# Column sums over features: high and low parts stacked on 64 partitions each, one pass with ones

## The reference

```python
def rmsnorm(x, w):
    return x * jax.lax.rsqrt(jnp.mean(x * x, axis=-1, keepdims=True) + EPS) * w
def film(x, cond, w, b):
    scale, shift = jnp.split(cond @ w + b, 2, axis=-1)
    return x * (1.0 + scale[:, None, :]) + shift[:, None, :]
h = film(rmsnorm(x, norm1_w), cond, film1_w, film1_b)
Q, K, V = h @ q_w + q_b, h @ k_w + k_b, h @ v_w + v_b
attn = softmax(einsum('bnd,bmd->bnm', Q, K) * 512 ** -0.5)
x = x + (einsum('bnm,bmd->bnd', attn, V) @ proj_w + proj_b)
h = film(rmsnorm(x, norm2_w), cond, film2_w, film2_b)
out = x + (gelu(h @ mlp_w1 + mlp_b1) @ mlp_w2 + mlp_b2)
```

## Time and profile before

| | us |
|---|---|
| median of 3 timed runs | 1762.76 (1762.69 to 1762.88) |
| profiled execution, its own time | 1765.63 |
| its span, first to last instruction | 1763.8 |
| TensorE busy | 1750.1 (99%) |
| VectorE busy | 1254.7 (71%) |
| ScalarE busy | 888.1 (50%) |
| GpSimd busy | 205.7 (12%) |

### The profile page before, as it was taken

The page is one execution under the profiler, slowest core; times in us unless marked ns, Lnnn a source line. Parts: engine busy times, 40 slices in busy tenths (PEclk is TensorE's granted clock), DMA queues, the critical chain, the costliest instruction groups (busy, mean ns, idle before and its releaser), DMA issues.

```text
span 1763.8 us, 23169 instructions
## 1 busy us (share of the span) xinstructions
PE 1750.1 (99%) x8308; PEld 1468.9 (83%) x8308; DVE 1254.7 (71%) x1749; ACT 888.1 (50%) x1490; POOL 205.7 (12%) x202
## 2 busy tenths in 40 slices
PE   8899999999999999999999999999999999999998
PEld 7788888888888888888888888888888888888887
DVE  5867677565665787588578758858875885885476
ACT  5454545545454555455455445545544554653344
POOL 0578685000000000000000000000000000000000
PEclk9999999999999999999999999999999999999999
DMA  9586868633226678768777866876786677677675
GB/s 335 163 297 249 291 256 274 245 99 112 78 102 199 201 250 277 207 203 276 249 197 250 280 202 207 274 248 197 262 267 201 220 269 243 191 244 240 193 233 194
DMA packets 202307, 395.83 MB, mean 224 GB/s; under 512 B 24145, under 2 KB 28241, under 8 KB 200145
## 3 DMA queue, kind: packets, MB, share of 16 engines
q1 hardware_dynamic: 202192, 394.34, 68.8%
HBM read 331.25 MB, written 62.98 MB: 224 GB/s over the span
## 4 chain that ended last, share of the span: by engine, by line
PE 96%; DMA 2%; DVE 1%; ACT 1%; SPq 0%; POOL 0%; issue 0%; DVEq 0%
PE psum L687 35%; PE psum L707 23%; PE psum L587 14%; PE psum L715 12%; PE psum L657 3%; PE psum L615 3%; PE psum L616 3%; PE psum L620 3%; DMA norm_row<-rs_scratch 1%; DMA rs_scratch<-rstd 1%; DMA x_tok<-x_dram 1%; DVE h L1053 0%; ACT x_tok L803 0%; PE psum L601 0%; PE psum L648 0%; DVE h L1046 0%
## 5 line engine op out<-in xcount | busy, mean ns | idle before, releaser
L687 PE MATMUL psum<-op_hi_P,ring 128*128 128x512 f32 x1792 | 552.0, 389 | 0.0
L707 PE MATMUL psum<-stage_hi,ring 128*128 128x512 f32 x1792 | 442.5, 389 | 0.0
L707 PEld LDWEIGHTS psum<-stage_hi,ring 128*128 128x128 f32 x1792 | 336.3, 188 | 69.8
L687 PEld LDWEIGHTS psum<-op_hi_P,ring 128*128 128x128 f32 x1792 | 336.1, 188 | 69.6
L888 ACT CAST stage_hi<-x 128x1024 fp32r<-128x1024 f32 x224 | 235.4, 1054 | 235.2 <-PE psum L707 223.0
L687 PE MATMUL psum<-op_lo_P,ring 128*128 128x512 f32 x896 | 348.6, 389 | 0.0
L1266 DVE TENSOR_TENSOR stage_lo<-x,stage_hi 128x1024 fp32r<-128x1024 f32 x224 | 273.6, 1225 | 72.3 <-ACT stage_hi L888 72.1
L872 ACT ACTIVATE x<-x,vecs 128x512 f32<-128x512 f32 x192 | 138.1, 723 | 283.9 <-DVE x L1253 283.9
L715 PE MATMUL psum<-stage_lo,ring 128*128 128x512 f32 x896 | 239.5, 389 | 0.0
L687 PEld LDWEIGHTS psum<-op_lo_P,ring 128*128 128x128 f32 x896 | 168.2, 188 | 35.0
L715 PEld LDWEIGHTS psum<-stage_lo,ring 128*128 128x128 f32 x896 | 168.2, 188 | 34.9
(11 more groups left out here) (154 smaller groups left out, 2240.4 us busy)
## 6 DMA issues: line engine op xcount, KB each, us to landing
ring<-wu_scratch SPq DMA_DIRECT2D x448, 256.0 KB, 3.1
ring<-wd_scratch SPq DMA_DIRECT2D x448, 256.0 KB, 2.9
x_tok<-x_dram SPq DMA_DIRECT2D x16, 1024.0 KB, 10.9
xT_in<-xT_dram SPq DMA_DIRECT2D x16, 1024.0 KB, 8.2
x2T_scratch<-xT_in SPq DMA_DIRECT2D x32, 512.0 KB, 3.4
hn<-x2T_scratch SPq DMA_DIRECT2D x32, 512.0 KB, 5.6
xres<-x2T_scratch SPq DMA_DIRECT2D x32, 512.0 KB, 5.0
out_dram<-xres SPq DMA_DIRECT2D x32, 512.0 KB, 4.4
```

The source lines that it names most:

```text
L687: mm = pe.matmul(to, wt, b, start=q in FRESH and t == 0, stop=t == len(steps) - 1, skip_group_check=True)
L707: mm = pe.matmul(bank(q, dt), a[:, dt, part, :], stage_hi[r][:, e, :], start=q in FRESH and ss == 0 and e == 0 and part == 0, stop=False, ...
```

## The change

After the last accumulation VectorE now folds the upper 64 partitions onto the lower 64: one more addition, of 64x512 for the key terms and of 64x1024 for the sums of squares, which waits for the operation before it. A wait for the fold itself stands behind it at the end of `key_terms` and of `add_squares`. ScalarE casts the folded 64 partitions into the lower half of one tile (`key_halves`, `sq_halves_*`), and VectorE writes the low part into the upper half of the same tile. TensorE then sums both with one matmul with ones instead of two. `key_terms` no longer waits for `key_row_full`, since the low part has left the memory of `key_bias`.

```diff
@@ -631,7 +632,7 @@
                 pe.wait_ge(key_hi_done, n + 1)
                 pe.wait_ge(key_lo_done, n + 1)
                 wait_used(pe, pT_read, n)
-                product(pT, [(ones_r[:], key_hi[:]), (ones_r[:], key_lo[:])], key_row_full)
+                product(pT, [(ones_r[:], key_halves[:])], key_row_full)
 
             def scores(n):
                 pe.wait_ge(g_read, GB * n + GB)
...
@@ -658,13 +659,13 @@
                                    start=True, stop=True)
                 mm.then_inc(out_full, 1)
 
-            def sum_features(m, hi, lo, into):
+            def sum_features(m, halves, into):
 
                 pe.wait_ge(sq_hi_done, m + 1)
                 pe.wait_ge(sq_lo_done, m + 1)
                 for f in range(2):
                     t = slice(TOK * f, TOK * f + TOK)
-                    product(into[f], [(ones_r[:], hi[:, t]), (ones_r[:], lo[:, t])], stat_full if f == 1 else None)
+                    product(into[f], [(ones_r[:], halves[:, t])], stat_full if f == 1 else None)
 
             def up(p, jj, q):
                 s, w = jj % 2, stream(p, 0, 7 * jj + UP_ORDER.index(q))
...
@@ -820,9 +821,9 @@
                 nc.scalar.copy(h_hi[m % 2][:, k, :], h[m % 2][:, k, :]).then_inc(h_hi_done, 1)
 
             def key_high(n):
-                act.wait_ge(key_done, KD * n + KD)
+                act.wait_ge(key_done, (KD + 1) * n + KD + 1)
                 wait_used(act, key_row_full, n)
-                nc.scalar.copy(key_hi[:], key_bias[:]).then_inc(key_hi_done, 1)
+                nc.scalar.copy(key_halves[0:HALF_P, :], key_bias[0:HALF_P, :]).then_inc(key_hi_done, 1)
 
             def keep_g(n, j):
                 act.wait_ge(g_full, GB * n + j + 1)
...
@@ -845,9 +846,9 @@
                     act.wait_ge(hn_loaded[k], 16 * m + 16)
                     nc.scalar.activation(into[:, k, :], hn[:, k, :], ACT.Square).then_inc(sq_done, 1)
 
-            def sums_high(m, squares, hi):
-                act.wait_ge(sq_added, 3 * m + 3)
-                nc.scalar.copy(hi[:], squares[:, 0, :]).then_inc(sq_hi_done, 1)
+            def sums_high(m, squares, halves):
+                act.wait_ge(sq_added, 4 * m + 4)
+                nc.scalar.copy(halves[0:HALF_P, :], squares[0:HALF_P, 0, :]).then_inc(sq_hi_done, 1)
 
             def keep_sums(m, source):
                 act.wait_ge(stat_full, m + 1)
...
@@ -1062,18 +1063,21 @@
             def key_terms(n):
 
                 hn_, kb = h[n % 2], key_bias
-                wait_used(dve, key_row_full, n)
                 dve.wait_ge(h_done_act, 2 * n + 2)
                 dve.wait_ge(h_done_dve, 2 * n + 2)
                 dve.tensor_scalar(kb[:], hn_[:, 0, :], wq_bk[:, 0:1], bq_bk[:], ALU.mult, ALU.add).then_inc(key_done, 1)
                 for k in range(1, KD):
-                    dve.wait_ge(key_done, KD * n + k)
+                    dve.wait_ge(key_done, (KD + 1) * n + k)
                     dve.scalar_tensor_tensor(kb[:], hn_[:, k, :], wq_bk[:, k:k + 1], kb[:], ALU.mult,
                                              ALU.add).then_inc(key_done, 1)
+                dve.wait_ge(key_done, (KD + 1) * n + KD)
+                dve.tensor_tensor(kb[0:HALF_P, :], kb[0:HALF_P, :], kb[HALF_P:P, :], ALU.add).then_inc(key_done, 1)
+                dve.wait_ge(key_done, (KD + 1) * n + KD + 1)
 
             def key_low(n):
                 dve.wait_ge(key_hi_done, n + 1)
-                dve.tensor_tensor(key_lo[:], key_bias[:], key_hi[:].bitcast(F32), ALU.subtract).then_inc(key_lo_done, 1)
+                dve.tensor_tensor(key_halves[HALF_P:P, :], key_bias[0:HALF_P, :], key_halves[0:HALF_P, :].bitcast(F32),
+                                  ALU.subtract).then_inc(key_lo_done, 1)
 
             def key_column(n):
 
...
@@ -1095,12 +1099,17 @@
                 dve.wait_ge(sq_done, KD * m + 4)
                 dve.tensor_tensor(squares[:, 0, :], squares[:, 0, :], squares[:, 1, :], ALU.add).then_inc(sq_added, 1)
                 dve.tensor_tensor(squares[:, 2, :], squares[:, 2, :], squares[:, 3, :], ALU.add).then_inc(sq_added, 1)
-                dve.wait_ge(sq_added, 3 * m + 2)
+                dve.wait_ge(sq_added, 4 * m + 2)
                 dve.tensor_tensor(squares[:, 0, :], squares[:, 0, :], squares[:, 2, :], ALU.add).then_inc(sq_added, 1)
-
-            def sums_low(m, squares, hi, lo):
+                dve.wait_ge(sq_added, 4 * m + 3)
+                dve.tensor_tensor(squares[0:HALF_P, 0, :], squares[0:HALF_P, 0, :], squares[HALF_P:P, 0, :],
+                                  ALU.add).then_inc(sq_added, 1)
+                dve.wait_ge(sq_added, 4 * m + 4)
+
+            def sums_low(m, squares, halves):
                 dve.wait_ge(sq_hi_done, m + 1)
-                dve.tensor_tensor(lo[:], squares[:, 0, :], hi[:].bitcast(F32), ALU.subtract).then_inc(sq_lo_done, 1)
+                dve.tensor_tensor(halves[HALF_P:P, :], squares[0:HALF_P, 0, :], halves[0:HALF_P, :].bitcast(F32),
+                                  ALU.subtract).then_inc(sq_lo_done, 1)
 
             def scale_pair(m, ks):
                 dve.wait_ge(row2_loaded, 16 * m + 16)
```

More of the change, by code:

```diff
@@ L27 @@
 P = 128
+HALF_P = 64
 EPS = 1e-6
@@ L118, in cond_block_kernel @@
         sq_mlp = at(80, "sq_mlp", [P, KD, PAIR])
-        sq_hi_mlp, sq_lo_mlp = at(84, "sq_hi_mlp", [P, PAIR], F32R), at(88, "sq_lo_mlp", [P, PAIR], F32R)
+        sq_halves_mlp = at(84, "sq_halves_mlp", [P, PAIR], F32R)
         hn = at(96, "hn", [P, KD, PAIR])
@@ L162, in cond_block_kernel @@
         probs, pT_sb = at(88, "probs", [P, GB, P]), at(90, "pT_sb", [P, TOK])
-        key_bias, key_lo = at(92, "key_bias", [P, TOK]), at(92, "key_lo", [P, TOK], F32R)
-        key_hi = at(94, "key_hi", [P, TOK], F32R)
+        key_bias = at(92, "key_bias", [P, TOK])
+        key_halves = at(94, "key_halves", [P, TOK], F32R)
         xT_in = [at(kb, f"xT_in{r}", [P, KD, TOK]) for r, kb in enumerate((168, 128, 176))]
@@ L172, in cond_block_kernel @@
         sq_attn = at(112, "sq_attn", [P, KD, PAIR])
-        sq_hi_attn, sq_lo_attn = at(116, "sq_hi_attn", [P, PAIR], F32R), at(120, "sq_lo_attn", [P, PAIR], F32R)
+        sq_halves_attn = at(116, "sq_halves_attn", [P, PAIR], F32R)
         tmix_attn = [at(4 * i, f"tmix_attn{i}", [P, 2, TOK]) for i in range(3)]
@@ L752, in _ @@
                     pe.wait_ge(bias_done, n + 1)
-                    sum_features(0, sq_hi_attn, sq_lo_attn, sums_attn)
+                    sum_features(0, sq_halves_attn, sums_attn)
                 v_product(n, 2)
@@ L791, in _ @@
                             pe.wait_ge(up_u2, HALF * p + 2)
-                            sum_features(p + 1, sq_hi_mlp, sq_lo_mlp, sums_mlp)
+                            sum_features(p + 1, sq_halves_mlp, sums_mlp)
                 for q in DOWN_ORDER:
@@ L966, in _ @@
                     if n == 10:
-                        sums_high(0, sq_attn, sq_hi_attn)
+                        sums_high(0, sq_attn, sq_halves_attn)
             for p in range(PAIRS):
@@ L989, in _ @@
                     if jj == 1 and more:
-                        sums_high(p + 1, sq_mlp, sq_hi_mlp)
+                        sums_high(p + 1, sq_mlp, sq_halves_mlp)
                     if jj in (5, 6) and more:
@@ L1199, in _ @@
                 if n == 11:
-                    sums_low(0, sq_attn, sq_hi_attn, sq_lo_attn)
+                    sums_low(0, sq_attn, sq_halves_attn)
                 if n == 13:
@@ L1316, in _ @@
                     if jj == 1 and more:
-                        sums_low(p + 1, sq_mlp, sq_hi_mlp, sq_lo_mlp)
+                        sums_low(p + 1, sq_mlp, sq_halves_mlp)
                     dve.wait_ge(slot_done, up_slot(p, jj, "P3"))
```

## The result

| | before | after |
|---|---|---|
| median, measured side by side | 1763.23 us (7 runs, 1762.69 to 1765.78) | 1768.56 us (7 runs, 1767.2 to 1771.93) |
| profiled execution, its own time | 1765.63 | 1767.59 |
| its span | 1763.8 | 1765.8 |

The ratio is 1.0031, interval 1.0021 to 1.0041: the change makes the kernel slower by 0.31%, +5.3 us. Forecast were 1766.6, or +3.8. 32 matmuls are gone, 8308 to 8276, and the time is longer.

The account below looks back on a forecast made before the run. TensorE, 99% busy, was taken as the bound. Removed matmuls -7.0, squares' fold +8.8 and key fold +2.0 gave +3.8 us: 1769.4 on the profiled execution, 1766.6 as median, range 1763.2 to 1768.8.

Parts of the forecast that it names:

- A: The forecast: both folds make TensorE wait; 1766.6 us, own range 1765.0 to 1768.2, chance 57%.
- Removed matmuls, −7.0: Key rows and sums on TensorE: 32 matmuls with ones go, 31 of them worth 0.227 us each, 7.0 us gained.
- The squares' fold, +8.8: MLP: fold of 1.22 us delays joins u, v and product P4, costing 1.26 us a pair, seven times.
- the 1.1 to 1.3: Sign in TensorE's list of waits: new entry L688 on `vsum`, 7 times, 1.1 to 1.3 us each.
- The rule on waits: VectorE's chained operations: semaphores cost nothing extra; by it the squares' loss is near 7 us, the sum about +2.
- The key fold, +2.0: Attention groups 3 to 7: fold waits for GpSimd, delaying `add_output`; 5 x 0.4 us, between 0 and 4.5.
- The start and groups 8 to 15, nothing: Attention: key fold fits VectorE's idle time in groups 8 to 15; group 0's first cast slips about 0.1; cost 0.
- B: Rival: only the squares' fold makes TensorE wait, key fold hidden in all groups; +1.8, 1764.5 us, chance 27%.
- C: Rival: the squares' fold is covered, TensorE shows no wait on `vsum`; 1755.7 us, faster, chance 9%.
- the room of v: MLP, before P4 of step 1: join v could end at most 0.25 us later before TensorE waits.
- D: Rival: TensorE's stops halve its clock afterwards, some 1.6 us each, seven times, 11 us more; 1777.8 us, chance 7%.
- The chances: Whole kernel, edge at 3.5 us: slower 0.50, same 0.41, faster 0.09, taking three quarters of A's range as slower.

Follow-up runs that it names:

- an addition alone: Kernel before plus an unused 64x1024 VectorE addition behind the third addition of squares in the MLP, no matmul removed: MLP 1237.09 us, +8.35.
- the key half alone: Kernel before with only the key terms folded and stacked, the sums of squares left as they were: 1764.1 us, ratio 1.0003.
- gaps twice as long: Kernel before plus two unused 64x1024 VectorE additions in a row behind the third addition of squares in the MLP: MLP 1253.81 us, +25.1.

## Why the prediction came out right

The forecast (A, both folds make TensorE wait) is what happened: 1768.56 against 1766.6. That is just above A's own range (to 1768.2) and inside the stated one (to 1768.8). The sum is 1.5 short, and one term of it, the key fold, is why; 0.4 of the squares' term went the other way. Side by side the kernel before was also 0.5 slower than the 1762.76 that the forecast was added to.

**Removed matmuls, −7.0.** Right: −7.1 when nothing else changes.

**The squares' fold, +8.8.** The mechanism is right: the fold takes the full 1.22, and u, v and P4 slip one behind the other. The size is 8.4 in the changed kernel and 8.35 as an addition alone, 1.19 a pair in place of 1.26, but that it lies so near is in part luck. The wait was forecast at 1.18 and is 1.04. Of the difference, 0.06 is the third wait, in front of u, which cost nothing beyond an ordinary dependent start (699.60 + 1.22 to 700.86, 0.04 in place of 0.10), so that u came 2.52 and not 2.58 after the third addition's start; 0.08 is the step from v's end to P4, which takes 0.06 and not the 0.14 read at the first key row, so that v had 0.33 of room and not 0.25. Against that, the restart costs 0.15 and not 0.08: not only the first interval behind a wait is longer (0.34 in place of 0.227), the next ones are by some hundredths too. These two errors cancel. TensorE's list shows 0.9 for each wait and not the 1.1 to 1.3 that the prediction named as a sign.

**The rule on waits** (the Trainium skill, "VectorE: DVE Perf Modes", section "The DRAIN you can't avoid": a semaphore after each chained operation costs nothing extra). It would have made the term near 7. In the changed kernel the pair without a wait again takes about 0.11 less from start to start: 1.14 (695.95 to 697.09), and 1.25 and 1.26 with one. The rows decide: the wait is not free, though it is small.

**The key fold, +2.0.** This is the term that was mis-sized: 3.6 in the changed kernel, and 5.0 with the key half alone, which is above its upper bound of 4.5. Two steps failed. I took the other engines' times from the trace of before and let the fold meet the cast in group 7; it met the subtraction in front of it, in that group and in groups 2 to 6 too, and took 1.66 to 1.67. And I gave groups 1 and 2 room; in the changed kernel group 2 lost 0.22, with the key half alone group 1 lost 1.18. How near it was, an estimate from the earlier trace rows says: `add_output` 0 ended at 289.87 and the output started at 290.79, so there were 0.86 us of room, and a fold of 0.69 moves `add_output` by some 0.8 (0.69, its two waits of 0.03 to 0.04, and the 0.08 that the start 289.13 lay ahead of the key terms' end at 289.21). Unstretched it would just have fitted; at 1.67 it doesn't. That it takes both, the fold at this place and GpSimd beside it, two runs show: with GpSimd's work cut the loss in groups 2 to 7 is gone, and with the fold behind `add_output` it is gone as well. The rule of the Trainium skill, "SBUF — State Buffer", section "Who interferes with whom" (an exclusive lock for a whole instruction), agrees: 0.69 us of work ended 1.67 after it started, behind the end of GpSimd's subtraction, while the additions of outputs, with one input in PSUM, took 1.41 for two, 1.40 before.

**The start and groups 8 to 15, nothing.** Groups 8 to 15 are right; free groups are 29.65 in place of 29.89. In group 0 the fold delays the first key row by more than the 0.1 of the prediction: it takes 0.69 in front of the cast, and TensorE waits 3.2 in place of 2.1. Whether any of it reaches the end can't be told within the scatter of the start.

**The rivals.** B (the key fold hidden) is refuted by the five waits in front of L658. C (covered) needed the squares' fold inside the room of v; it takes 1221 ns, and even the 0.61 of half the data would not have fitted. C's 1755.7 also leaves the key fold at nothing. D (the clock): it stayed at 1.00 behind the 1.27 gaps,

```profile
704.00:707.00 3.00, 3.00 (x15) 2.47 (x14) 2.60 (x3) 2.21 (x4) 0.00 (x0) 1.00 0.55 150
```

the stretch of the changed kernel behind the gap at 701.13. But D was the right thing to price: with gaps twice as long it came, five times in seven, at the 1.6 us each that had been worked out from the start. The argument against D was weaker than it looked, since of the two waits of 1.8 us in the start one was followed by the full clock and one by the lower.

**The chances.** One step in them is wrong. Of A's range, +2.2 to +5.4, the part above 3.5 is 1.9 of 3.2, six tenths and not three quarters. With it slower has 0.34 + 0.07 = 0.41 and the same 0.23 + 0.27 = 0.50, so the prediction leaned to slower by a slip.

**What stays open.** Why VectorE's and GpSimd's instructions meet differently in the changed kernel and in the one with the key half alone: I read the meetings from the traces, and could not have worked them out from the one before. Both kernels have one profile each here, so how far these 3.6 and 5.0 vary from run to run is not known either. Why the first and the last of the seven long gaps left the clock alone is open too.

## What to carry to other kernels

Where TensorE is at 99%, a trade of its work for VectorE's is decided by where the new instruction stands in VectorE's list: count back from the matmul that waits next, and put the instruction behind the last operation that it waits for. The same two folds cost 12.0 us of waits (3.6 and 8.4) in front of these operations and none to speak of (under 0.1) behind them. Folding partitions saves nothing on VectorE; it adds a whole instruction of the same free size. And a busy share (71% here) says nothing of room at a place; the idle time in brackets in front of the next operations does.

## What the runs showed of the hardware

- The count of partitions made no difference to VectorE's time: 64x1024 takes 1221 ns and 128x1024 1.22 us; 64x512 686 ns and 128x512 0.69 us, also with the two inputs on different halves of the partitions. 64x64 takes 0.22 us.
- The clock fell to 0.50 at a stop of 2.14 us idle (2.53 from start to start) in five cases of seven, and never after 0.88 (1.27) in the seven of the changed kernel. The slow matmuls began between 0 and 1.1 us after the restart, seven or eight of them, and cost 1.6 us beyond the stop. In the start 1.84 us idle brought it on in one run and 2.24 did not in another.
- The first interval between two matmuls behind a wait is 0.34 in the MLP (the earlier trace rows has 0.31) in place of 0.227, and the whole restart costs 0.15.
- From the end of VectorE's operation to the start of the matmul that waited for it, 0.06 us in the dense stretches (702.34 to 702.40), where the earlier trace rows has 0.14 at the first key row.
- A fold of 0.69 us took 1.66 to 1.67 beside a subtraction of GpSimd of 1.62, and 0.98 beside the end of a cast; it ended 0.54 to 0.55 after the instruction that it met.
- The overlap of matmuls hides a short stop from the list of waits: a loss of 0.20 us a pair, 1.4 us in all, left no line there.
